# First attention of a four-block network: the router's steps of a quad of tiles put into one pair, and the first statistics and roots moved ahead

## The reference

```python
def _L0_attn_a_ref(x, head_dim_mask, w_q, w_k, w_v, w_o):
    q, k, v = x @ w_q, x @ w_k, x @ w_v          # einsums over the features
    scores = jnp.einsum('bqd,bkd->bqk', q, k) * scale
    h = jnp.einsum('bqk,bkd->bqd', jax.nn.softmax(scores, axis=-1), v)
    return (h * head_dim_mask) @ w_o
...
# the mixture of experts: E = 8 experts, the best two for each token
logits = x @ router_w
idx1 = jnp.argmax(gates, axis=-1)
idx2 = jnp.argmax(gates * (1.0 - mask1), axis=-1)
pos1 = jnp.cumsum(mask1, axis=0) - mask1
pos2 = jnp.cumsum(mask2, axis=0) - mask2 + jnp.sum(mask1, axis=0, keepdims=True)
```

## Time and profile before

| | us |
|---|---|
| median of 3 runs | 833.57 |
| the profiled execution | 834.5 |
| its span, first to last instruction | 832.8 |
| PE busy in the span | 758.8 (91%) |
| DVE busy | 493.7 (59%) |
| ACT busy | 440.6 (53%) |
| POOL busy | 431.7 (52%) |
| mean granted clock of TensorE, of full speed | 0.971 |

### The profile page before, as it was taken

One profiled execution on the slowest core, in us unless ns is written; L12 is line 12 of the kernel. 1 busy time (PEld: TensorE's weight loads), 2 busy tenths in 40 slices (PEclk: granted clock), 3 DMA queues, 4 the chain that ended last, 5 costly groups with the idle time before them and its releaser, 6 DMA issues. The chain is left out here.

```text
span 832.8 us, 18726 instructions
## 1 busy us (share of the span) xinstructions
PE 758.8 (91%) x6472; PEld 688.7 (83%) x6472; DVE 493.7 (59%) x1626; ACT 440.6 (53%) x1071; POOL 431.7 (52%) x545
## 2 busy tenths in 40 slices
PE   5877789699999997999999999999989599999994
PEld 4777789599999995777877787877779599999994
DVE  4777864245444455767777777867666244444437
ACT  2545455144444443676767766776655144444456
POOL 3347777155555551334344665665576255555530
PEclk9999979799999999999999999999999799999999
DMA  7981111233333224233223342223111233334138
GB/s 258 317 346 53 48 42 55 67 101 99 96 116 102 71 89 124 84 106 114 77 78 94 109 128 91 81 84 98 37 39 41 68 87 101 96 98 127 53 91 233
DMA packets 78164, 87.42 MB, mean 105 GB/s; under 512 B 12744, under 2 KB 66602, under 8 KB 77944
## 3 DMA queue, kind: packets, MB, share of 16 engines
q1 hardware_dynamic: 67872, 68.60, 26.7%
q0 software_dynamic: 9216, 17.34, 6.1%
q10 hardware_dynamic: 984, 0.29, 0.2%
HBM read 48.59 MB, written 39.65 MB: 106 GB/s over the span
## 5 line engine op out<-in xcount | busy, mean ns | idle before, releaser
L1172 ACT ACTIVATE hT<-bank,bias_T 128x256 f32<-128x256 f32 x448 | 175.5, 475 | 216.4 <-PE bank L815 216.3
L545 POOL DMA_INDIRECT y_rows<-yo,row_cur x160 | 157.7, 985 | 147.1 <-DVE yo L1662 119.0
L1752 DVE TENSOR_REDUCE negp<-bank 128x2 f32<-128x512 f32 (+1 forms) x192 | 128.3, 687 | 70.4 <-PE bank L879 67.4
L836 PE MATMUL bank<-w_s,hT 128*128 128x128 f32 x1280 | 156.0, 275 | 0.0
L530 POOL DMA_INDIRECT x_slots<-xr,slot_u x128 | 129.4, 1011 | 41.3 <-issue 33.9
L836 PEld LDWEIGHTS bank<-w_s,hT 128*128 128x128 f32 x1280 | 150.1, 192 | 0.0
L583 POOL TENSOR_SCALAR_AFFINE_SELECT pt<-pt 128x512 f32<-128x512 f32 x128 | 79.4, 642 | 124.2 <-ACT pt L1232 124.0
L1232 ACT ACTIVATE pt<-bank 128x512 f32<-128x512 f32 x192 | 107.7, 596 | 60.4 <-PE bank L907 50.6
L815 PE MATMUL bank<-xT_hl,w_hl 128*128 128x256 f32 x960 | 136.3, 292 | 3.5 <-DVE w_hl L1635 2.7
L815 PEld LDWEIGHTS bank<-xT_hl,w_hl 128*128 128x128 f32 x960 | 121.6, 193 | 4.2 <-DVE w_hl L1635 3.1
L1662 DVE TENSOR_TENSOR yo<-bank,b_b 128x256 f32<-128x256 f32 x80 | 34.0, 425 | 146.4 <-PE bank L836 146.4
(11 more groups left out here) (205 smaller groups left out, 1263.0 us busy)
## 6 DMA issues: line engine op xcount, KB each, us to landing
xg<-x_slots SPq DMA_DIRECT2D x80, 136.0 KB, 2.1
w_s<-in_L_ffn_w SPq DMA_DIRECT2D x32, 256.0 KB, 3.2
qk_rows<-qks SPq DMA_DIRECT2D x16, 512.0 KB, 4.0
bdk<-qk_rows SPq DMA_DIRECT2D x192, 32.0 KB
qc<-qk_rows SPq DMA_DIRECT2D x48, 128.0 KB, 2.9
x_slots<-xg SPq DMA_DIRECT2D x1, 5440.0 KB, 21.2
y_rows<-xg SPq DMA_DIRECT2D x1, 4096.0 KB, 16.2
bdk<-y_rows SPq DMA_DIRECT2D x1, 4096.0 KB
```

What stands on the lines that cost most here:

```text
L545: pool.indirect_dma_start(y_rows, bass.IndirectOffsetOnAxis(ap=row_cur[:, g % ROWS, j:j + 1], axis=0), yo[:, g % RING, j, :], None, bounds ...
L836: m = pe.matmul(yb(w, l)[:, j * P:(j + 1) * P], hT[:, w % 2, f, j * P:(j + 1) * P], wt[:, f, :], start=(f == 0), stop=(f == FT - 1))
L1172: a = act.activation(hT[:, w % 2, f, :], HB[2 * (w % 2) + f // 2][:, (f % 2) * 256:(f % 2) * 256 + 256], ACT.Silu, bias=bias_T[:, b0 + f:b ...
L1752: dve.tensor_reduce(dst, AB[(g + k) % 2][:, :].rearrange("p (j k) -> p j k", j=heads), AX.X, ALU.max, negate=True).then_inc(S.amax_done, 1)
```

## The change

Five things are moved; no arithmetic is added or taken away.

1. The second choice of quad i-1 (`second`, eight steps) is made in pair i, directly behind its first choice, in the gaps between `stats2`, `add_attn` and `stats2_end`. The slots of quad i-2 (`placed`) move from the second half of pair i to its first half, between the steps of `norm_r`, and `norm` now lies between the steps of `lead`. `add_attn(n)` comes behind `placed` and `norm_r`.
2. PE makes the counts of quad i-2 directly behind the scores of sequence n+1, ahead of the projection of n+2, the values of n and a transpose. The logits go ahead of the projection of n+3.
3. ACT copies the router's transposes ahead of the transposed probabilities, and `gate_exps` comes directly behind `exps(n+2)`.
4. The eight first statistics are done by pair 1 (before: by pair 2), and seven of their roots stand ahead of the first `rstd2_of`. `split_sw1` moves from the end of pair 0 into pair 6.
5. POOL starts 4 dispatches ahead of the root of pair 2 where it started 2, and 7 for each pair as before.

```diff
--- before.py
+++ after.py
@@ -547,16 +547,14 @@
                                             ).then_inc(sca[g % RING], 16)
 
             def attn_a():
-                for q in range(5):
+                for q in range(7):
                     rstd_of(q, q + 1)
                 rstd2_of(1)
-                rstd_of(5, 6)
-                rstd_of(6, 7)
+                rstd_of(7, 8)
                 rstd2_of(2)
-                rstd_of(7, 8)
                 done = 0
                 for i in range(2, PAIRS):
-                    upto = 2 + DISPATCHED * (i - 2)
+                    upto = 4 + DISPATCHED * (i - 2)
                     for k in range(done, upto):
                         dispatch(0, k)
                     done = upto
@@ -739,14 +737,14 @@
                     a_probs_transpose(n)
                 if 0 <= n + 1 < SEQS:
                     a_scores(n + 1)
+                if valid(i - 2):
+                    counts(i - 2, KK_)
                 if 0 <= n + 2 < SEQS:
                     a_project(n + 2)
                 if valid(i):
                     a_values(n)
                 if 0 <= n + 3 < SEQS:
                     a_transpose(n + 3)
-                if valid(i - 2):
-                    counts(i - 2, KK_)
                 if valid(i - 1):
                     r_transpose(i - 1)
 
@@ -754,10 +752,10 @@
                     a_probs_transpose(n + 1)
                 if 0 <= n + 2 < SEQS:
                     a_scores(n + 2)
+                if valid(i - 1):
+                    r_logits(i - 1)
                 if 0 <= n + 3 < SEQS:
                     a_project(n + 3)
-                if valid(i - 1):
-                    r_logits(i - 1)
                 if valid(i):
                     a_values(n + 1)
                 if 0 <= n + 4 < SEQS:
@@ -1139,20 +1137,20 @@
                 if 0 <= n + 3 < SEQS:
                     xnT_copy(n + 3)
 
+                if valid(i - 1):
+                    r_copy(i - 1)
                 if valid(i):
                     p_copy(n + 1)
-                if valid(i - 1):
-                    r_copy(i - 1)
                 if 0 <= n + 3 < SEQS:
                     g_copy(n + 3)
                 if 0 <= n + 2 < SEQS:
                     exps(n + 2)
+                if valid(i - 1):
+                    gate_exps(i - 1)
                 if 0 <= n + 3 < SEQS:
                     v_copy(n + 3)
                 if 0 <= n + 4 < SEQS:
                     xnT_copy(n + 4)
-                if valid(i - 1):
-                    gate_exps(i - 1)
 
             for i in range(-2, PAIRS):
                 attn_a_pair(i)
@@ -1555,55 +1553,70 @@
 
             def attn_a_pair(i):
                 n = 2 * i
+                routed, led = valid(i - 2), valid(i - 1)
                 if valid(i):
                     inverse_sums(n)
                 if 0 <= n + 1 < SEQS:
                     maxes(n + 1)
-                if valid(i - 2):
-                    for k in range(4):
-                        second(i - 2, k)
+                for j in range(PLACED):
+                    if routed:
+                        placed(i - 2, j, bank[2])
+                    if led and j < 4:
+                        norm_r(i - 1, j)
+                if i == 0:
+                    stats(4, 5)
                 if valid(i):
                     add_attn(n)
-                for j in range(4):
-                    if valid(i - 2):
-                        second(i - 2, 4 + j)
-                    if valid(i - 1):
-                        norm_r(i - 1, j)
                 if i < 0:
                     dve.wait_ge((S.x_head, S.x_second)[i + 2], 16)
-                if i <= 2:
-                    stats(max(i, 0) + i + 2 + (i >= 0), max(i, 0) + i + 3 + (i >= 0))
+                    stats(i + 2, i + 3)
+                if 0 <= i <= 1:
+                    stats(2 * i + 5, 2 * i + 6)
 
                 if valid(i):
                     inverse_sums(n + 1)
                 if 0 <= n + 2 < SEQS:
                     maxes(n + 2)
-                if -1 <= i <= 1:
+                if -1 <= i <= 0:
                     if i == -1:
                         dve.wait_ge(S.x_tail, 16)
-                    stats(2 * i + 4, 2 * i + 5)
-                for j in range(PLACED):
+                    stats(4 * i + 6, 4 * i + 7)
+                for j in range(LEAD):
+                    if led:
+                        lead(i - 1, j)
                     if valid(i + 2) and i > -2 and j < 4:
                         if j == 0:
                             need(dve, S.xn_tr, 2 * i + 4)
                         norm(i + 2, i + 3, j)
-                    if valid(i - 2):
-                        placed(i - 2, j, bank[2])
+                if i == -1:
+                    stats(3, 4)
+                if led:
+                    second(i - 1, 0)
+                    second(i - 1, 1)
                 if valid(i):
                     stats2(i, 0)
-                if valid(i - 1):
-                    for k in range(LEAD):
-                        lead(i - 1, k)
+                if led:
+                    second(i - 1, 2)
+                    second(i - 1, 3)
+                if i == PAIRS - 2:
+                    split_sw1()
                 if i == PAIRS - 1:
                     x_split(0, 0)
                     x_split(0, 1)
                 if valid(i):
                     add_attn(n + 1)
+                if led:
+                    second(i - 1, 4)
+                if valid(i):
                     dve.wait_ge(S.attn_added, n + 2)
                     stats2(i, 1)
+                if led:
+                    second(i - 1, 5)
+                if valid(i):
                     stats2_end(i)
-                if i == 0:
-                    split_sw1()
+                if led:
+                    second(i - 1, 6)
+                    second(i - 1, 7)
 
             for i in range(-2, PAIRS):
                 if i == -1:
@@ -1667,9 +1680,6 @@
                 for w in range(start, upto):
                     c = w - FRONT[l]
                     if w == start:
-                        if l == 0:
-                            for k in range(SECOND):
-                                second(last - 1, k)
                         for j in range(4):
                             norm_r(last, j)
                     if w + 1 < ITEMS and not (l == 0 and w == 0):
```

## The result

| | before | after |
|---|---|---|
| median | 833.96 us (831.84 to 835.04, 4 runs) | 826.58 us (825.74 to 828.02, 4 runs) |
| profiled execution | 834.5 | 826.94 |
| its span | 832.8 | 825.1 |
| mean granted clock | 0.971 | 0.973 |
| POOL busy / DVE busy / PE busy | 431.7 / 493.7 / 758.8 | 431.0 / 491.7 / 757.5 |

The changed kernel takes 0.9917 of the time of the one before, with a 95% interval of 0.9898 to 0.9936: 7.4 us less by the medians, where the prediction had 3.0 us. An unedited copy in another series gave 826.50 against 833.32 us, 0.9931 (0.9910 to 0.9951), so by the medians the gain is 6.8 to 7.4 us.

What follows compares the result with a forecast made beforehand. POOL's row of dispatches was taken to bound the first 150 us; -2.7 (fewer dispatches) and -0.3 (last pairs) gave -3.0 us, 834.5 to 831.5 profiled, median 0.9 lower at 830.6 us, range 827.0 to 835.5.

Steps and rivals of the forecast that it cites:

- the term for the last pairs: Up to the last root's statistics: pairs end 2.1 us earlier, 1.8 us more work follows; net 0.3 us earlier.
- the clock behind the hand-over: PE's half clock after waiting for the first chunk: nothing in the sum; up to 3.2 us back in a rival, chance 0.14.
- What bounds the start: First 150 us: POOL's dispatches set the end, at DVE's last statistics plus the root plus the 27 dispatches left behind it.
- Fewer dispatches: POOL behind the last root: 25 dispatches in place of 27, 2 x 1.35 = 2.7 us less.
- The condition: POOL's early batches: the quad's slots must be there in time, first dispatch near 47 us, root not needed before 55 us.
- Early work: Start of the attention: statistics moved ahead cost 0, split_sw1 leaving pair 0 is credited 0.4 us.
- The pair's first half: From acc to the maxima of sequence n+2: DVE idles for 1.65 us where it idled 2.0.
- The second half: From the maxima to DVE's second choice in each pair: a new wait of 0.85 us.
- The falls in pairs 5 and 2: Half clock in the old pairs, 0.8 us in pair 5 and 1.2 in pair 2; none taken in pairs 2 to 6.
- the slower loop: Rival: the DVE and PE loop becomes the bound, 839 us, mostly near 836.5, decisive from pairs of 11.7 us; chance 0.14.
- more frequent falls: Rival: the clock falls as often as now, each costing more, two in pairs 2 to 6, 833.3 us; chance 0.27.
- More than forecast: Rival: clock stays up behind the first-chunk wait, 827.4 us, or pairs come down to 10.45 us, 827.6 us; chance 0.14.

Runs made afterwards that it cites:

- the grouping alone: Kernel before with only the dispatches grouped as 4, 11, 18 in place of 2, 9, 16: 837.63 us, ratio 1.0057.
- the filled kernel: Kernel before with six unread matmuls ahead of the wait for the counts of each pair: 831.24 us, ratio 0.9971; on disturbed chips 1.0064 and 1.0037.
- the fillers: Changed kernel with 20 unread matmuls ahead of pair 7's counts and 24 ahead of the first chunk's transposes: 828.58 us, ratio 0.9944.

## Why the prediction was wrong

The step that failed is the term for the last pairs, "Net 0.3 us earlier". The last root came 1.6 to 2.5 us earlier: 0.4 to 1.3 up to mark A, and 1.2 from A to C. A second one is the clock behind the hand-over, which the sum had at nothing: it gave 1.2 us. Part by part:

- **What bounds the start** was right: the last statistics, the root, the dispatches left behind it. With 27, 25 and 23 left, the first chunk moves as this says.
- **Fewer dispatches**: 2.7 us predicted. C to the first chunk's transposes went from 41.07 to 38.14 us: 2.9 us. In it the row of dispatches is 3.3 us shorter (two fewer, and 1.32 instead of 1.35 us each), and 0.4 us more pass between the last one and the transposes. The condition held as put: the first dispatch at 46.09 (near 47 forecast), the root behind four of them waits 1.93 us for its statistics. The run of the grouping alone shows what it costs where the condition fails.
- **Early work**: 0.4 us predicted, 0.4 to 1.3 found at A where the clocks of the start were alike, and some 0.3 to 0.5 more in the pair behind it (10.70 instead of 11.00 and 11.16). The 1.9 us between the two profiled executions at A are mostly the start's own spread.
- **The pair's first half**: 1.65 us of idle time predicted, 1.39 measured. **The second half**: a new wait of 0.85 us predicted, 0.80 measured. The sum gave 11.2, the steps laid one behind the other 10.95, and I took 11.1; measured were 10.74. The better number was the second one, and both stood on an old pair of 11.0 us, pair 6 of the profile, where two others took 10.8 and 10.7 (61.68 - 50.90, 72.36 - 61.68). With its waits filled the same pair 6 takes 10.68 us: the 11.0 still had 0.3 us of the fall in pair 5 in it, which the sum also counted by itself.
- **The falls in pairs 5 and 2**: 2.0 us predicted, and the filled kernel shows 56.45 - 54.00 = 2.45. The outcome and the size were right: waits of 1.6 us passed without a fall in five pairs. That the falls went because the waits are shorter is less sure than it looks, since the kernel before passed waits of 2.05 and 2.27 us without a fall, too. From the Trainium skill, "TensorE: Matmul & The Clock Gate", section "What's actually happening", I had concluded that falls would come as often as now; they didn't: from 40 to 96 us the changed kernel has none, the kernel before two. What the page states, that activity releases the clock, is not contradicted: fillers in the waits took the falls away.
- **The last pairs, net 0.3 us earlier**: the step that failed. By its own parts it was -0.4 up to A, 94.83 - 92.65 less those 0.4, so -1.8, from A to B, and +1.9 from B to C. Measured are -0.4 to -1.3, -2.75 (56.45 to 53.70) and +1.53 (17.23 to 18.76). Most is in A to B: 0.45 us by falls dearer than I had put them, 0.5 by the pairs, which I had 0 to 0.5 us longer in all and which are 0.3 shorter than the old ones at full clock. What stands behind pair 6 was nearly right. The half clock there costs 1.2 to 1.3 us in both kernels, and so drops out of the difference.
- **The clock behind the hand-over**: I put it into a rival with a chance of 0.14, "the wait is still the longest of the trace". The wait shrank to 2.61 us and not to 4.6, since the pieces ahead of it ended only 1.3 us earlier (145.8 to 144.45) where C came 3.1 earlier; I had let them move together. Then the half clock ended near 153 instead of 160 us, and 1.2 us came back (C to D is 4.14 less, the first chunk 2.93). It is not a separate case but follows from the shorter wait: the second term that failed.

Together: -0.4 to -1.3 (to A), -1.2 (A to C), -2.9 (first chunk), -1.2 (second chunk), -0.4 (behind it) are -6.1 to -7.0 us, against medians 7.4 and 6.8 us apart in the two series. The forecast had the mechanism and -3.0. Of the rivals, the slower loop decided nothing (pairs of 10.75 us, decisive from 11.7), and more frequent falls didn't come. "More than forecast" came nearest in time (827.4 and 827.6 us), but neither of its parts happened as put: the clock did fall behind the wait (0.50 from 150 to 152 us), only for a shorter time, and the pairs didn't come down to 10.45 us. That its time is nearly the measured one is luck.

The best version run is the changed kernel with batches of six, 822.22 us.

## What to carry to other kernels

Where one engine's list holds both a long row of transfers and small steps that others wait for, count what is left behind the last such step: moving transfers ahead of it pays one for one, but only if their inputs are there early enough; the same edit alone cost 4.5 us here. A short wait of TensorE that is removed returns more than its length, since work at half clock behind it comes back too; add that to the same case, not to a rival. And compare marks from a common point in each execution, not from the start of the span, before a microsecond or two is explained.

## What was not expected of the hardware

- Two executions of one program differed by 2.7 us at 36 us of the span through the clock of the first 24 us alone (0.65 and 0.57 in two stretches, against 1.00 and 1.00).
- Half clock ahead of the last root seemed to cost nothing: A to C is 72.46, 72.49 and 72.50 us, where the clock fell 10.4 us ahead of C (the first run), 10.7 us (the copy) and 3.6 us (the fillers). It costs 1.2 to 1.3 us (3.71 against 2.44 us from the transposes to the logits; 17.23 against 16.06 from B to C), which the fillers of that run took away again, being 1.8 us longer than the wait. An edit that removes a cost and adds an equal one looks like a cost of nothing.
- In the old order waits of 2.25 and 2.28 us were followed by half clock, and one of 2.27 was not.
- On four of the chips some of ACT's copies began 0.8 to 5.3 us behind the matmuls that they copy, in nearly every pair behind 60 to 81 us (0.04 us elsewhere), and the same programs took 5 to 6% longer. Of the kernels that ran on both kinds of chip, batches of two went from 0.9973 to 1.0023 and 1.0025, and the filled waits from 0.9971 to 1.0064 and 1.0037.
